# Protein sums of a pair mixer: quarters of 128 rows by 128 contracted, their products issued among the next quarter's stream

## What is computed

```python
# layer 0: pairs are normalized, gated and projected first
pp = sigmoid(ln(protein_pair) @ gw2) * (ln(protein_pair) @ w2 + b2)   # 256 x 256 x 64
block1 = einsum('bikc,bkjc->bijc', pp, ab1)                           # 256 x 64 x 64
# layer 1: the raw pairs are used, no gate
block1 = einsum('bikc,bkjc->bijc', protein_pair, ab)
```

## Time and profile before

| | us |
|---|---|
| median of 3 runs (2681.09 to 2686.23) | 2685.96 |
| profiled execution | 2686.12 |
| its span, first to last instruction | 2684.4 |
| PE busy | 1917.1 (71%) |
| PE weight loads busy | 1674.4 (62%) |
| DVE busy | 1474.2 (55%) |
| ACT busy | 1216.0 (45%) |
| POOL busy | 1187.5 (44%) |

### The profile page before, as it was taken

One profiled execution on the slowest core, in us unless ns is written; L12 is line 12 of the kernel. 1 busy time (PEld: TensorE's weight loads), 2 busy tenths in 40 slices (PEclk: granted clock), 3 DMA queues, 4 the chain that ended last, 5 costly groups with the idle time before them and its releaser, 6 DMA issues. The chain is left out here.

```text
span 2684.4 us, 52043 instructions
## 1 busy us (share of the span) xinstructions
PE 1917.1 (71%) x12902; PEld 1674.4 (62%) x12903; DVE 1474.2 (55%) x6291; ACT 1216.0 (45%) x3261; POOL 1187.5 (44%) x1255
## 2 busy tenths in 40 slices
PE   6867877777683200008999999937699557999996
PEld 5756767666573200006888888835499347998995
DVE  7966584774895411113333333359622896776666
ACT  4566483663561000004555555524310465776665
POOL 3544242331892677773555555556510671001220
PEclk9988998999675555558999999967799678999998
DMA  4022231321730311112222222145562210000003
GB/s 130 0 64 76 67 106 52 94 78 34 282 129 1 105 53 51 53 52 76 71 70 71 70 71 69 45 140 165 136 156 65 80 47 7 0 0 1 0 0 126
DMA packets 248341, 193.95 MB, mean 72 GB/s; under 512 B 94328, under 2 KB 210358, under 8 KB 248254
## 3 DMA queue, kind: packets, MB, share of 16 engines
q1 hardware_dynamic: 230846, 159.08, 20.4%
q0 software_dynamic: 17408, 33.87, 3.5%
HBM read 123.09 MB, written 71.86 MB: 73 GB/s over the span
## 5 line engine op out<-in xcount | busy, mean ns | idle before, releaser
L1420 POOL DMA_INDIRECT choices<-ab_tiles x288 | 287.3, 998 | 255.2 <-ACT ab_tiles L1454 181.7
L315 POOL TENSOR_TENSOR small<-small 128x4 f32<-128x4 f32 x192 | 199.0, 1037 | 331.3 <-DVE small L308 331.3
L1334 POOL DMA_INDIRECT sorted_tokens<-work x256 | 248.0, 969 | 121.0 <-issue 80.9
L1491 PE MATMUL banks<-w,hidden 128*128 128x128 f32 x2304 | 276.3, 278 | 0.0
L1491 PEld LDWEIGHTS banks<-w,hidden 128*128 128x128 f32 x2304 | 262.6, 192 | 16.3 <-ACT hidden L1445 16.1
L1468 PE MATMUL banks<-ident,ab_tiles 128*128 128x128 f32 x288 | 44.0, 277 | 308.5 <-DMA ab_tiles<-sorted_tokens 308.5
L344 PE MATMUL banks<-ident,small 128*128 128x128 f32 x640 | 124.5, 313 | 182.2 <-ACT small L332 151.6
L1548 PE MATMUL banks<-small 128*128 128x128 f32 x1536 | 239.9, 293 | 6.4 <-DVE small L1603 3.8
L1468 PEld LDWEIGHTS banks<-ident,ab_tiles 128*128 128x128 f32 x288 | 34.5, 144 | 309.0 <-DMA ab_tiles<-sorted_tokens 308.8
L332 ACT ACTIVATE small<-small 128x128 f32<-128x128 f32 x384 | 161.6, 484 | 144.2 <-DVE small L320 143.9
L1541 PE MATMUL banks<-ab_tiles,small 128*128 (+1 forms) x1536 | 215.1, 277 | 6.2 <-DMA small<-L_ffn_V_o 6.2
(11 more groups left out here) (223 smaller groups left out, 4924.0 us busy)
## 6 DMA issues: line engine op xcount, KB each, us to landing
small<-L_conv_protein_pair SPq DMA_DIRECT2D x128, 256.0 KB
sorted_tokens<-work SPq DMA_DIRECT2D x32, 585.0 KB
ab_tiles<-sorted_tokens SPq DMA_DIRECT2D x72, 260.0 KB, 2.8
work_again<-choices SPq DMA_DIRECT2D x32, 512.0 KB, 3.8
work_again<-L_conv_protein_pair SPq DMA_DIRECT2D x32, 512.0 KB, 6.1
x_tiles<-x SPq DMA_DIRECT2D x32, 256.0 KB, 3.7
work<-x SPq DMA_DIRECT2D x32, 256.0 KB, 3.1
after_mixture<-x_tiles SPq DMA_DIRECT2D x32, 256.0 KB, 2.2
```

The costliest lines, as they stand in the source:

```text
L315: self.scaled.done(pool.tensor_tensor(self.r[:, u, :], self.var[:, u, :], self.mhalf, ALU.pow))
L1334: pool.indirect_dma_start(out=self.sorted, out_offset=bass.IndirectOffsetOnAxis(ap=where[:, u, t, k:k + 1], axis=0), in_=rows[:, u, t, k, ...
L1420: pool.indirect_dma_start(out=self.out, out_offset=bass.IndirectOffsetOnAxis(ap=rows[:, u, t, E + 1:ROW].bitcast(U32), axis=0), in_=y[:, u ...
L1491: last = pe.matmul(out[:, t * P:(t + 1) * P], hidden[:, u % 2, h, t * P:(t + 1) * P], w2[:, u % 2, h * P:(h + 1) * P], start=False, stop=h ...
```

## The change

Both layers now work on quarters q = ic * 2 + kc: 128 rows i by 128 contracted k. A product is one matmul with 128 stationary columns instead of two with 64, its output covers all 128 partitions, and nothing accumulates in PSUM over kc; DVE adds both quarters of a row block to the sums, 32 adds as before, of 128 x 512 instead of 64 x 512 values. Loads have the same number, bytes and runs of 256 bytes.

In layer 0 the products of quarter q are issued among the stream of quarter q + 1: PE's loop has a third stage with lag 37 that issues 3 channels' products per group (22 of 32 groups), DVE's has a fourth stage with lag 38 that adds a bank. All loops of DVE, ACT and PE are written out in full (`peel` is the whole length).

```diff
 def chunk_buffers(chip):
-    return Carve(chip.work)(2, ICS, C, C)
+    return Carve(chip.work)(2, P, C)

+PER_GROUP = 3
+BLOCK_LAG = 37
 def protein_sums(nc, chip, tag, par, raw_pairs, chunk_in=None):
-    per_chunk = ICS * C // G
+    per_chunk = P // G
+    quarters = ICS * ICS
...
+        last_of = [-(-8 * (c8 + 1) // PER_GROUP) - 1 for c8 in range(C // 8)]
+        def product(pe, q, c):
+            kc = q % ICS
+            return pe.matmul(chip.banks[:, 4 + c // 8 % 4, c % 8 * NC_:(c % 8 + 1) * NC_],
+                             buffer(q)[:, :, c], chip.ab[:, kc * NC_:(kc + 1) * NC_, 0, c], start=True, stop=True)
+        def accumulate(dve, ic, n, c8):
+            sums = chip.ab[:, bass.ds(ic * NC_, NC_), 1, c8 * 8:(c8 + 1) * 8]
+            blocked.ready(dve, n)
+            summed.done(dve.tensor_tensor(sums, chip.bank(4 + c8 % 4).rearrange("p (c j) -> p j c", c=8), sums, ALU.add))
...
             def _(dve):
-                            engine_loop(dve, per_chunk, 4, [(lambda m, u: stream.stats(dve, base + m, u), 0),
-                                                            (lambda m, u: stream.apply(dve, base + m, u), 1), (gate, 4)])
-                        for c8 in range(C // 8):
-                            blocked.ready(dve, n)
-                            summed.done(dve.tensor_tensor(
-                                sums, chip.banks[rows, 4 + c8 % 4, :].rearrange("p (c j) -> p j c", c=8), sums, ALU.add))
+                def add_blocks(n, u):
+                    q, r = n // per_chunk, n % per_chunk
+                    if r in last_of:
+                        accumulate(dve, q // ICS, q * 8 + last_of.index(r), last_of.index(r))
+                engine_loop(dve, quarters * per_chunk, 4,
+                            [(lambda n, u: stream.stats(dve, n, u), 0), (lambda n, u: stream.apply(dve, n, u), 1),
+                             (lambda n, u: stream.gate(dve, dest(n), n, u), 4), (add_blocks, BLOCK_LAG + 1)],
+                            peel=quarters * per_chunk)
...
             def _(pe):
-                            engine_loop(pe, per_chunk, 4, [(lambda m, u: stream.norm.turn(pe, base + m, u), 0),
-                                                           (lambda m, u: stream.project(pe, base + m, u), 1)])
-                            stream.gated.ready(pe, base + (per_chunk - 1))
-                        for c8 in range(C // 8):
-                            summed.free(pe, n)
-                            for cc in range(8):
-                                for kc in range(ICS):
-                                    last = pe.matmul(chip.banks[h * C:(h + 1) * C, 4 + c8 % 4, cc * NC_:(cc + 1) * NC_],
-                                                     pp[:, 1 - h, kc, :, c], chip.ab[:, kc * NC_:(kc + 1) * NC_, 0, c],
-                                                     start=kc == 0, stop=kc == ICS - 1)
+                def block_products(n, u):
+                    q, r = n // per_chunk, n % per_chunk
+                    if r == 0:
+                        stream.gated.ready(pe, (q + 1) * per_chunk - 1)
+                    for c in range(r * PER_GROUP, min(C, (r + 1) * PER_GROUP)):
+                        if c % 8 == 0:
+                            summed.free(pe, q * 8 + c // 8)
+                        last = product(pe, q, c)
+                        if c % 8 == 7:
                             blocked.done(last)
+                engine_loop(pe, quarters * per_chunk, 4,
+                            [(lambda n, u: stream.norm.turn(pe, n, u), 0), (lambda n, u: stream.project(pe, n, u), 1),
+                             (block_products, BLOCK_LAG)], peel=quarters * per_chunk)
```

More of the change, by code:

```diff
@@ L590, in chunk_buffers, with load_chunk @@
 def chunk_buffers(chip):
-    return Carve(chip.work)(2, ICS, C, C)
-def load_chunk(sp, pp, ppv, ic, h, arrived):
-    for kc in range(ICS):
[L596 to L599, removed]
+    return Carve(chip.work)(2, P, C)
+def load_chunk(sp, pp, ppv, ic, kc, arrived):
+    for i in range(0, P, ROWS):
+        sp.dma_start(pp[:, 1 - kc, i:i + ROWS, :],
+                     ppv[ic * P + i:ic * P + i + ROWS, kc * P:(kc + 1) * P, :]
+                     .rearrange("i k c -> k i c")).then_inc(arrived, 16)
 def compound_sums(nc, chip, tag, par, raw_pairs):
@@ L737, in protein_sums, with buffer, dest @@
         summed = Flow(chip, "summed", 4)
-        def where(m, u, h):
-            kc = u % 2
-            return kc, (m - kc) * 2
+        last_of = [-(-8 * (c8 + 1) // PER_GROUP) - 1 for c8 in range(C // 8)]
+        def buffer(q):
+            return pp[:, 1 - q % ICS]
+        def dest(n):
+            i = (n % per_chunk) * G
+            return buffer(n // per_chunk)[:, i:i + G, :]
+        def product(pe, q, c):
[6 more added lines that the diff above has]
+            summed.done(dve.tensor_tensor(sums, chip.bank(4 + c8 % 4).rearrange("p (c j) -> p j c", c=8), sums, ALU.add))
         with nc.Block() as block:
@@ L747, in _ @@
                 if raw_pairs:
-                    for q in range(1, 2 * ICS):
+                    for q in range(1, quarters):
                         blocked.free(sp, q * 8 + 7)
-                        load_chunk(sp, pp, ppv, q // 2, q % 2, pp_in[q % 2])
+                        load_chunk(sp, pp, ppv, q // ICS, q % ICS, pp_in[q % 2])
                     return
@@ L753, in _ @@
                 with sp.Fori(0, ICS) as ic:
-                    for h in range(2):
+                    for kc in range(ICS):
                         def load(m, u):
-                            kc, i = where(m, u, h)
-                            src = ppv[bass.ds(ic * P + (i + h * C), G), kc * P:(kc + 1) * P, :]
-                            stream.load(sp, [(0, src.rearrange("i k e -> k i e"))], (ic * 2 + h) * per_chunk + m, u)
+                            src = ppv[bass.ds(ic * P + m * G, G), kc * P:(kc + 1) * P, :]
+                            stream.load(sp, [(0, src.rearrange("i k e -> k i e"))], (ic * 2 + kc) * per_chunk + m, u)
                         engine_loop(sp, per_chunk, 4, [(load, 0)])
@@ L764, in _ @@
                     stream.norm.open_pool(pool)
-                    engine_loop(pool, 4 * per_chunk, 4, [(lambda n, u: stream.norm.rstd(pool, n, u), 0)])
+                    engine_loop(pool, quarters * per_chunk, 4, [(lambda n, u: stream.norm.rstd(pool, n, u), 0)])
             @block.vector
@@ L769, in _ @@
                 summed.open(dve)
[L770 to L780, removed]
-                            engine_loop(dve, per_chunk, 4, [(lambda m, u: stream.stats(dve, base + m, u), 0),
-                                                            (lambda m, u: stream.apply(dve, base + m, u), 1), (gate, 4)])
-                        rows = slice(h * C, (h + 1) * C)
-                        for c8 in range(C // 8):
-                            n = (ic * 2 + h) * 8 + c8
-                            sums = chip.ab[rows, bass.ds(ic * NC_, NC_), 1, c8 * 8:(c8 + 1) * 8]
-                            blocked.ready(dve, n)
-                            summed.done(dve.tensor_tensor(
-                                sums, chip.banks[rows, 4 + c8 % 4, :].rearrange("p (c j) -> p j c", c=8), sums, ALU.add))
+                if raw_pairs:
+                    with dve.Fori(0, ICS) as ic:
+                        for kc in range(ICS):
+                            for c8 in range(C // 8):
+                                accumulate(dve, ic, (ic * 2 + kc) * 8 + c8, c8)
+                    return
+                stream.gated.open(dve)
+                stream.lin.fold(dve)
+                def add_blocks(n, u):
[6 more added lines that the diff above has]
+                            peel=quarters * per_chunk)
             @block.scalar
@@ L795, in _, with squash @@
                 stream.norm.open_act(act)
[L796 to L805, removed]
+                def squash(n, u):
+                    blocked.free(act, n // per_chunk * 8 + 7)
+                    stream.squash(act, dest(n), n, u)
+                engine_loop(act, quarters * per_chunk, 4,
+                            [(lambda n, u: stream.apply_act(act, n, u), 0),
+                             (lambda n, u: stream.keep(act, n, u), 1), (squash, 2)], peel=quarters * per_chunk)
             @block.tensor
@@ L809, in _ @@
                 blocked.open(pe)
[L810 to L820, removed]
-                            engine_loop(pe, per_chunk, 4, [(lambda m, u: stream.norm.turn(pe, base + m, u), 0),
-                                                           (lambda m, u: stream.project(pe, base + m, u), 1)])
-                            stream.gated.ready(pe, base + (per_chunk - 1))
-                        for c8 in range(C // 8):
-                            n = (ic * 2 + h) * 8 + c8
-                            summed.free(pe, n)
-                            for cc in range(8):
-                                c = c8 * 8 + cc
-                                for kc in range(ICS):
```

(24 more changed lines are left out.)

## The result

| | before | changed |
|---|---|---|
| median, us | 2683.53 (4 runs, 2680.47 to 2686.23) | 2717.07 (4 runs, 2716.38 to 2718.01) |
| profiled execution, us | 2686.12 | 2716.38 |
| its span, us | 2684.4 | 2714.7 |
| ratio | | 1.0124, 95% interval 1.0108 to 1.014 |

What follows compares the result with a forecast made beforehand. Layer 0's phase was taken as the sum of DVE's stream and PE's product bursts, which don't overlap. Terms: 2686.1 - 6 (layer 0 at full clock) + 48 (clock) - 4 (layer 1) = 2724 us; range 2635 to 2768.

Steps and rivals of the forecast that it cites:

- The pitch c: Time per record of the new strided 128-column product, both layers: 0.21 us, making layer 1 4 us shorter.
- The wait: Layer 0 stream: 24 adds each wait a full trip, PE idle 3.42 us, 10.65 us between adds; phase 6 us shorter.
- The clock: Layer 0 stream: PE's clock drops after each of 24 idles, 2.0 us lost per add, +48 us.
- Costed at nothing: DVE's 128-partition adds, loads, written-out loops (bounds -8 to +10 us) and ACT's semaphore per quarter, all set to 0.
- E: Rival on the products' pitch: c is 0.26 us, 13.4 us per add, total 2773 us; chance 0.12.
- B: Rival on the products: load isn't the limit, pitch 0.111 to 0.146 us, total 2633 to about 2659 us; chance 0.18.
- C: Rival on layer 0's stream: PE's clock holds through idles of 3.4 us, total 2676 us; chance 0.10.
- D: Rival on layer 0: products and adds disappear in the stream, adds find their bank ready, total 2591 us; chance 0.06.
- F: Rival: the parts cancel, c near 0.17 or fewer clock drops, total within 5 us of 2686; chance 0.06.

Runs made afterwards that it cites:

- Experiment 5: Changed kernel with each product's stationary operand 128 neighbouring floats instead of 128 floats 256 bytes apart, giving other sums; 2672.39 us (one run).
- experiment 6: Changed kernel with each product's moving operand 64 neighbouring floats instead of 64 floats 512 bytes apart, giving other sums; 2711.33 us (one run).
- experiment 3: Changed kernel with 11 unread identity matmuls (fillers) issued on PE behind each group that fills a bank; 2683.85 us, ratio 0.9993 to the kernel before.
- experiment 1: Changed kernel with DVE's lag for the add raised from 38 to 41, three groups later; 2602.41 us, ratio 0.9686 to the kernel before.
- experiment 4: Changed kernel's quarters and 128-column products, but in bursts behind each quarter's stream, with the loops of the kernel before; 2678.93 us, ratio 0.9978.

## Why the prediction was right

It said 2724, 38 us more; measured 2717, 33 us more (the profiled executions: 30). The mechanism, a wait in every add and a clock that falls behind it, is what the runs show. That the number came so close is in part luck: the clock's term was 17 us too high, and the others together 10 too low. Step by step:

- **The pitch c.** 0.21 from the rows, 0.217 measured; a load takes 310 ns where the sum had 306. Experiment 5 shows that the stationary operand's stride doubles it and experiment 6 that the moving one has no part. Layer 1 was put at -4 and came to -0.6. The Trainium skill's page "TensorE: Matmul & The Clock Gate", section LDWEIGHTS, says that the column count sets the time of a load. That was the better guide here: by it 2 x 0.111 = 0.222 is an estimate of the pitch, and the trace agrees within 3%. The column count is not all, though: 128 neighbouring columns go at 0.112.
- **The wait.** Forecast: 24 idles of DVE released by PE, PE idle 3.42 us on average, 10.65 us between adds at full clock. Measured in the first quarter: PE idle 2.83 to 3.70 behind the banks, 10.56 between adds with the clock held up (experiment 3). DVE's own idle was guessed at about 3 each; it is 4.0 on average with the clock held up and 5.1 in the changed kernel, so the guess was 1 us short, and what the clock takes from PE is another 1.1. Moving the lag and nothing else takes 115 us away (experiment 1).
- **The clock.** Forecast +48 (2.0 per add), measured 1.33 per add, 31 us. This is the term that was mis-sized. A likely reason is visible in the timeline: the rows it was taken from hold no strided product, and these take 1.39 us for 6 records at half clock and 1.44 at full; only the transposes and projections, half of the work, lose.
- **Costed at nothing.** The written-out loops: bounds -8 to +10, set to 0 (the +10 comes from no row); the kernel before with them is 7 us slower, so part of the 33 may be theirs. The first quarter of the changed kernel went at 2.30 us a group, against 2.26 before. The adds of 128 partitions: 0.69 us, as before.
- **What evened out.** The end of the phase was forecast at 654.6 + 48 = 702.6 and came at 692.5. The clock's term is 17 us too high. Against it stand 2.2 us at the start of group 32 (301.6 for 299.4) and some 4.5 for the rest of the phase at full clock: with the fillers it runs from 299.1 to 658.8, 359.7 us for the 355.2 of the sum, 1.1 of them in the last burst (28.0 for 26.9). Layer 1 brought 3 us less than forecast.
- **A slip.** The prediction counts 1.125 products left behind a bank's last one. A quarter's last group has only one product, so the mean is 7 / 8 = 0.875, and the idle of PE was put 0.1 us too short. E's idle of 3.34 is 3.30 by the prediction's own way. Neither matters.
- **The rivals.** B (the load isn't the limit) fell with the row of layer 1. Experiment 5 makes B's pitch real: its 11.25 us per add came true in layer 0 (11.24), but not its -49 in layer 1, where the clock fell. C (the clock holds) fell: the clock is 0.83 in the stream. D needed adds that find their bank ready; the code's order didn't let them. E's pitch of 0.26 was not reached, and F (the parts cancel) fell with the 33 us.

## What to carry to other kernels

When an in-order engine gets a new consumer stage in a software pipeline, lay its lag beside the position of the producer's stage in the other engine's iteration: a consumer that waits for something behind the newest item's own work drains all engines, and one item of lag more may give back nearly all of it (93 of 115 us here). Count stationary columns and their stride before halving a number of products: here, with strided float32 columns, the load set the pace, and the columns cost the same in products of 64 or of 128 (0.111 and 0.217 us a record). And measure interleaved work with the idle that it leaves: here idles of 3 us cost PE's clock on top of themselves, 31 us in all.

## What the runs showed of the hardware

**A busy PE whose granted clock falls.** In layer 1 the changed kernel's PE is busy without a gap for 111 us and is granted half the clock for all but the first 2 us, where the kernel before has 0.98 over its 64-column products. Windows of the changed kernel, then of the kernel before:

```profile
2001.60:2112.60 111.00, 111.00 (x512) 111.00 (x512) 21.44 (x31) 0.00 (x0) 0.00 (x0) 0.50 0.50 114
```

```profile
1967.80:2079.60 111.80, 111.80 (x1024) 111.63 (x1024) 21.35 (x31) 0.00 (x0) 0.00 (x0) 0.98 0.50 113
```

So does a burst of experiment 4 in layer 0, 0.54 over 28 us. What brings the clock down there no run shows. These products themselves don't feel it, but experiment 5 shows that it can matter: once down, the clock did not come back in 80 us of gapless 128 x 64 products. A busy share of 100% was no promise of full clock.

**A load whose pace doesn't follow the clock.** Products with the strided stationary load keep their pitch: 0.217 at 0.50 in layer 1 (111.2 / 512), and 0.215 at 1.00 in experiment 1's stream (2.62 a group less 1.33 for transposes and projection, over 6 records). With neighbouring floats the pitch is 0.112 at full and 0.212 at half clock. The Trainium skill's page "SBUF — State Buffer", section "Door 1: The DMA port swizzle", says that SBUF is read in lines of 16 bytes, that each access which crosses to a new line pays a penalty, and that a float32 operand can therefore step by up to 4 values for free. The strided load, 64 values a step, agrees with that (0.217 against 0.112 at full clock); the strided moving operand of 64 columns showed no cost under the longer load.
